# Global attention of a four-layer kernel: value products of two key tiles placed together on every second step

## What is computed

```
q, k, v = h @ W_query[n], h @ W_key[n], h @ W_val[n]     # per head n: (2, 1024, 8)
p       = exp(q @ k.T / sqrt(8) - rowmax)                # (1024, 1024) per batch and head
o       = (p @ v) / sum(p)                               # sum over keys
y       = sum over n of o[n] @ W_out[n]
```

## Time and profile before

| | |
|---|---|
| median of 3 runs | 3236.36 us (3233.23 to 3241.91) |
| the profiled execution, its own time | 3240.98 us |
| span of its trace | 3239.0 us |
| mean granted TensorE clock over the span | 0.915 |
| busy: PE, DVE, ACT, POOL | 2859.6, 2317.0, 1971.7, 1207.8 us |
| global attention in the trace | about 1119 to 1577 us |

### The profile page before, as it was taken

The page is one execution under the profiler, slowest core; times in us unless marked ns, Lnnn a source line. Parts: engine busy times, 40 slices in busy tenths (PEclk is TensorE's granted clock), DMA queues, the critical chain, the costliest instruction groups (busy, mean ns, idle before and its releaser), DMA issues.

```text
span 3239.0 us, 87872 instructions
## 1 busy us (share of the span) xinstructions
PE 2859.6 (88%) x36340; PEld 1714.1 (53%) x36340; DVE 2317.0 (72%) x3906; ACT 1971.7 (61%) x5614; POOL 1207.8 (37%) x851
## 2 busy tenths in 40 slices
PE   4769869475979799999689999999999999999997
PEld 3534557342334423333256666666666666666664
DVE  4840266447950577777589888888888888888885
ACT  3531265135422256666468887888778887888785
POOL 0010000100000011111157766766776676676662
PEclk7579855698989889999889999999999999999999
DMA  2000000000000200000223233232332332322222
GB/s 105 3 1 0 37 2 4 1 1 0 0 0 0 63 20 23 23 23 23 94 56 77 65 78 92 66 76 67 99 79 67 99 78 67 99 64 62 61 66 51
DMA packets 48236, 153.37 MB, mean 47 GB/s; under 512 B 11552, under 2 KB 13856, under 8 KB 45952
## 3 DMA queue, kind: packets, MB, share of 16 engines
q1 hardware_dynamic: 47872, 148.17, 17.4%
HBM read 43.60 MB, written 5.44 MB: 15 GB/s over the span
## 4 chain that ended last, share of the span: by engine, by line
PE 71%; DVE 16%; ACT 7%; issue 2%; DVEq 2%; DMA 1%; POOLq 1%; ACTq 1%; SPq 0%; POOL 0%
PE ps L1506 13%; PE ps L673 7%; PE ps L1524 5%; PE ps L1559 5%; DVE arena L997 4%; PE ps L1101 4%; PE ps L1129 4%; PE ps L1568 4%; PE ps L1581 4%; PE ps L1116 3%; PE ps L1541 3%; PE ps L1550 2%; PE ps L1587 2%; PE ps L308 2%; DVE arena L1974 1%
## 5 line engine op out<-in xcount | busy, mean ns | idle before, releaser
L1506 PE MATMUL ps<-arena 128*128 128x512 f32 x1152 | 562.5, 611 | 17.4 <-ACTq L1793 16.1
L1858 ACT ACTIVATE arena<-ps,arena 128x64 f32<-128x64 f32 x1536 | 458.8, 318 | 86.8 <-DVE arena L2054 83.6
L2131 POOL TENSOR_TENSOR arena<-arena 128x1024 f32<-128x1024 f32 x190 | 447.5, 2361 | 97.9 <-DVE arena L1943 97.9
L2137 POOL TENSOR_TENSOR arena<-arena 128x2048 f32<-128x2048 f32 x95 | 344.3, 3624 | 224.5 <-ACT arena L1800 219.4
L1266 DVE TENSOR_REDUCE arena<-ps 128x1 f32<-128x512 f32 x512 | 329.5, 686 | 76.9 <-PE ps L1101 71.8
L1228 ACT ACTIVATE arena<-ps 128x1024 f32<-128x1024 f32 x256 | 262.2, 1024 | 178.3 <-PE ps L1116 177.8
L1858 ACT ACTIVATION_READ_ACCUMULATOR arena<-ps,arena 128x1 f32 x1536 | 323.3, 210 | 0.0
L1506 PEld LDWEIGHTS ps<-arena 128*128 128x128 f32 x1152 | 197.0, 191 | 182.3 <-issue 157.8
L191 POOL TENSOR_SCALAR rstd<-mv 128x4 f32<-128x4 f32 x32 | 7.9, 247 | 721.2 <-DVE mv L178 721.2
L1938 DVE TENSOR_TENSOR arena<-ps,arena 128x1024 f32<-128x1024 f32 x192 | 234.2, 1220 | 47.0 <-PE ps L1506 32.7
L1943 DVE TENSOR_TENSOR arena<-ps,arena 128x512 f32<-128x512 f32 x384 | 245.5, 681 | 0.0
(11 more groups left out here) (286 smaller groups left out, 5516.5 us busy)
## 6 DMA issues: line engine op xcount, KB each, us to landing
arena<-pack_l SPq DMA_DIRECT2D x144, 256.0 KB
arena<-grow SPq DMA_DIRECT2D x144, 256.0 KB
arena<-in_deep SPq DMA_DIRECT2D x6, 2649.5 KB, 10.8
arena<-pack_l SPq DMA_DIRECT2D x96, 128.0 KB
arena<-grow SPq DMA_DIRECT2D x84, 128.0 KB
arena<-in_rotary SPq DMA_DIRECT2D x6, 1024.0 KB, 7.5
pack_tern<-in_tern SPq DMA_DIRECT2D x2, 2888.0 KB, 10.5
arena<-scr_q SPq DMA_DIRECT2D x96, 48.0 KB
```

What stands on the lines that cost most here:

```text
L1506: last = T.matmul(m.ps[0:rows.stop - rows.start, at + half, :], f.xs[t % 2][:, rows], w.wqkv[:, j * INNER + half * BLK:j * INNER + (half + ...
L1858: last = A(f.prob[:, p, :], m.ps[:, 4 + j % 2, i * SPAN:(i + 1) * SPAN], ACT.Exp, bias=f.nmax[t % 2][:, p:p + 1], accum_out=f.rsum[t % 2][ ...
L2131: G.tensor_tensor(f.rot[t % 2][:, here], f.rot[t % 2][:, here], f.sin[:, here], ALU.add)
L2137: G.tensor_tensor(r, r, spread(f.ss[t % 2], DH), ALU.mult).then_inc(s["rotated"], 1)
```

## The change

Sub-steps with an even kt now have no V. Those with an odd kt have two sets, V(kt - 3) and V(kt - 2), and sub-step 1 has V(6) and V(7) of the pair before.

```diff
@@ -1146,10 +1146,12 @@
         before = pair_at(r, par, -1)
         for kt in range(BT):
             exponents(r, par, kt)
-            if kt >= 2:
+            if kt % 2 and kt >= 3:
+                values(r, par, kt - 3)
                 values(r, par, kt - 2)
-            elif not first:
-                values(*before, kt + BT - 2)
+            elif kt == 1 and not first:
+                values(*before, BT - 2)
+                values(*before, BT - 1)
             if kt == 0 and not first and not (last and par == RING - 1):
 
                 scores_job(*pair_at(r, par, LEAD - 1), 2 * BT)
```

## The result

The changed kernel takes 3281.85 us (3281.18 to 3282.93, 3 runs) against 3236.36: the ratio is 1.0134, with a 95% interval of 1.0119 to 1.0149. It is slower by 1.3%: the whole interval lies above 1. The forecast was 3281 us. The profiled execution took 3282.93 us with a span of 3281.2, 42.2 more than before.

What follows compares the result with a forecast made beforehand. TensorE was taken to bound the stage, VectorE close behind. Waits inside pairs (+0.43 a double sub-step) and at turns (+0.44) summed to +44 to +45 us, from 3236.4 to 3281 us; range 3264 to 3302.

Steps and rivals of the forecast that it cites:

- What bounds: Middle of the global attention: TensorE bounds, VectorE not far behind; the V between E and S exactly covers VectorE's time.
- The saving: Two sub-steps inside a pair: without any wait they would take 2.89 us instead of 3.12, 0.23 saved.
- Inside a pair: Two sub-steps take 3.55 us against 3.12, +0.43: 0.66 of waiting for VectorE less 0.23 saved.
- The turn: Between pairs: V(6) loses its free cover under T's wait for the maxima; S(14) to S(2) grows from 4.01, +0.44 us.
- The sum: A pair goes from 13.61 to 15.10 us, +1.49, 43.2 us over pairs 1 to 29; in all +44 to +45 us.
- Costed at nothing: Later `pv` against T and ScalarE's collect cost nothing; if either cover failed, under 10 us in all.
- Pair 0: First pair, no turn before it: three double sub-steps, less the hidden transposes, add +1.1 us.
- The rival with a lost clock: Holes in PE's work lose the high clock for a fifth of the stage: 46 us more, 3327 us; chance 3%.
- It cancels: VectorE releases banks early enough in even sub-steps, only the pair's turn costs: -0.25 us a pair, 3229 us; chance 4%.
- faster: Only the tiling mode changes count: 0.23 us less per double sub-step, 29 us less in all, 3207 us; chance 3%.
- The rule: Changing tiling mode drains TensorE; the change halves the drains between V and S or E, so it should pay.

Runs made afterwards that it cites:

- the short maxima: Row maxima over 128 of the 512 columns of each S: 3216.72 us in the order before, 3197.17 us in the changed order.

## Why the prediction was right

- **What bounds.** TensorE with VectorE close behind, the cover just as long as two reads: shown by the short maxima, where the same change turns from over 40 us slower into 19.6 us faster, and by sub-step 1, which takes as long without its V as with it.
- **The saving.** Predicted 2.89 us for a double sub-step without waits, from two rows and one distance (E to S) taken from its nearest row at 0.45. Measured 2.85, with 0.44 for S to E and E to S alike, and V to V at its lower bound: 1.07 for 16 records in the loop as at the stage's end.
- **Inside a pair.** Predicted waits until 1.18 and 1.78 and a double sub-step of 3.55; measured 1.17, 1.77 and 3.53.
- **The turn.** Predicted S(2) at 4.45 after S(14); measured 4.43. Alone, this half cost 0.36 us a pair by its T: 0.43 in the ordinary pairs and nearly nothing in those that were slow before. The prediction counted with the mean of 13.61 for every pair, and did not see that some stood out.
- **The sum.** Predicted 15.10 a pair and +44 to +45 us; measured 15.05, 42.2 on the profiled execution (3282.9 where 3286 was forecast) and 45.5 between the medians of 3 runs each. Against the kernel before as it ran beside the experiments (3240.55 and 3238.83) the change costs 41 and 43 us. So the sum is good to about 3 us, and that the median came within 1 us of 3281 is luck.
- **Costed at nothing.** The last two pairs, the later `pv` and the later stages: 0.6 us less from the last T on, and S waits for its operands from memory as long as before (7.4 us in both groups). Pair 0 was put at +1.1 and took +0.97, but by a slip: it has no transposes (the call of `turn` asks for `not first`) that could be hidden, so its own terms give +1.3.
- **The clock.** The rival with a lost clock did not come: the granted clock is 1.00 in the stretch in which PE is busy 46.12 of 54.00 us. *It cancels* and *faster* asked for a VectorE that finishes two reads sooner; built that way, the faster order came.
- **The rule.** By the Trainium skill ("TensorEngine Tiling (Array Packing)", Key Properties) a change of tiling mode drains TensorE. The trace agrees as far as it goes: from V to V it is 0.43 us, from V to S or E 0.57, and with short maxima the twos of V sets save 0.25 us a double sub-step (2.85 against 3.10). With whole reads the grouping also took away the cover of VectorE's reads, and that cost more than it saved.

## What to carry to other kernels

Before grouping work on the busiest engine, list what each piece covers: here the transfer of two buffers between two engines ran without waits only while the producer had other work of the consumer's length between its couples, and grouping that work emptied every second gap. Two buffers filled one at a time, with something between, ask for less cover than two filled in a burst; spreading them came first here, and only then did moving work into an idle place pay (nothing without it, 13 us with it). A distance between instructions that the trace lacks could here be taken from its mirror (S to E for E to S), and it does not matter at all where a wait covers it. A mean over the turns of a loop can hide one that differs: list the single ones before taking it as the cost of each.

## What the runs showed that I had not expected

The short row maxima saved another 6.6 us in the two pairs of S that run alone ahead of the first E: that stretch is VectorE's (24.36 us to the second pair's T, 17.75 with short reads), a separate place where this stage can be shortened. A maximum over 128 columns in place of 512 takes 291 ns in place of 686: (686 - 291) / 384 = 1.03 ns a column, and by a straight line through the two some 160 ns that do not depend on the columns (an estimate from these two rows).
